# The second layer's convolution: five products over 113 rows become four over 128

## The reference

```
xz = jnp.einsum('bhwc,ec->bhwe', xp, in_proj_w)          # 48 -> 2 x 96
x_in, x_gate = jnp.split(xz, 2, axis=-1)
xc = conv_general_dilated(x_in, conv2d_w, (1, 1), 'SAME', feature_group_count=96)   # 3 x 3
x_act = jax.nn.silu(xc).reshape(B, H * W, 96)
ym = _mamba(x_act, ...)
ym = ym.reshape(B, H, W, 96) * jax.nn.silu(x_gate)
out = jnp.einsum('bhwd,cd->bhwc', ym, out_proj_w)

# in _mamba, after products that make u, z, dt, B and C:
da = jnp.exp(dt_t[..., None] * A)
h = da * h + (dt_t * x_t)[..., None] * B_t[:, None, :]
y = jnp.einsum('bdn,bn->bd', h, C_t)                     # then (y + xm * Dp) * silu(z), out_w
```

## Time and profile before

| | |
|---|---|
| median of 3 runs | 1626.08 us (1622.43 to 1626.56) |
| profiled execution | 1625.65 us |
| its span in the profile | 1623.8 us |
| TensorE (PE) busy | 1286.5 us, 79% |
| VectorE (DVE) busy | 1271.7 us, 78% |
| ScalarE (ACT) busy | 1154.7 us, 71% |
| GpSimd (POOL) busy | 898.3 us, 55% |
| pair products, `m_qf` L1499 | 192 instructions, 124.4 us busy, 799 ns each |
| scans, `m_h` L1729 | 384 instructions, 463.8 us busy, 53.4 us idle before them |

### The profile page before, as it was taken

How to read it: one execution, slowest core, us unless ns; L and a number is a source line. 1 busy time by engine, 2 the same in 40 slices (tenths; PEclk the granted TensorE clock), 3 DMA queues, 4 the chain that set the end, 5 groups by cost and what they waited for, 6 DMA issues and landing times. The chain is left out here.

```text
span 1623.8 us, 14529 instructions
## 1 busy us (share of the span) xinstructions
PE 1286.5 (79%) x3822; PEld 436.9 (27%) x3822; DVE 1271.7 (78%) x1274; ACT 1154.7 (71%) x1691; POOL 898.3 (55%) x451
## 2 busy tenths in 40 slices
PE   4999757585763577768789988998989889776995
PEld 2444201010110355532122222222222222111663
DVE  1665659999996477730999999999999999894775
ACT  2677358687773477748898898889898988641564
POOL 2400037969788333313987787888787888750000
PEclk8999955555555799978788889888897898555998
DMA  5344480200101233225877787777787877634572
GB/s 153 106 137 124 109 183 0 84 20 1 52 1 63 68 97 98 83 56 149 193 180 171 183 190 175 175 174 182 167 183 181 187 172 162 132 71 105 130 175 67
DMA packets 136429, 200.54 MB, mean 123 GB/s; under 512 B 26739, under 2 KB 68770, under 8 KB 135564
## 3 DMA queue, kind: packets, MB, share of 16 engines
q1 hardware_dynamic: 133740, 196.15, 49.5%
q10 hardware_dynamic: 2160, 2.61, 0.6%
q0 software_dynamic: 448, 0.85, 0.2%
HBM read 145.93 MB, written 53.63 MB: 123 GB/s over the span
## 5 line engine op out<-in xcount | busy, mean ns | idle before, releaser
L1375 POOL TENSOR_TENSOR m_ub<-m_dlb,m_bt 128x1536 f32<-128x1536 f32 x128 | 440.2, 3441 | 144.1 <-DVE m_h L1729 136.8
L1729 DVE TENSOR_TENSOR_SCAN m_h<-m_qa,m_state,m_ub 128x512 f32<-128x512 f32 x384 | 463.8, 1262 | 53.4 <-POOL m_ub L1375 51.9
L1691 ACT ACTIVATE m_qa<-m_dlb,k_a 128x512 f32<-128x512 f32 x384 | 254.8, 684 | 107.9 <-DVE m_h L1729 102.0
L1097 POOL TENSOR_TENSOR b_u<-b_dl,b_z 128x1024 f32<-128x1024 f32 x48 | 125.2, 2608 | 212.0 <-DVE b_dl L1014 211.4
L1740 DVE TENSOR_TENSOR m_g<-m_h,m_qc 128x1536 f32<-128x1536 f32 x128 | 221.7, 1732 | 14.3 <-issue 7.7
L1558 PE MATMUL m_qc<-m_bcr,k_selc 32*128 32x512 f32 x256 | 167.5, 738 | 81.8 <-DVE m_g L1740 81.6
L1575 PE MATMUL m_qy<-m_g,k_seld 128*32 128x512 f32 x768 | 169.5, 743 | 0.0
L944 PE MATMUL b_qb<-b_bc,k_pack_sel 96*128 96x512 bf16 x96 | 81.6, 850 | 73.6 <-DVE b_u L1020 71.0
L1499 PE MATMUL m_qf<-m_cva,k_conv 113*96 113x504 f32 (+1 forms) x192 | 124.4, 799 | 5.0 <-PEq L1131 5.0
L1558 PEld LDWEIGHTS m_qc<-m_bcr,k_selc 32*128 32x128 f32 x256 | 42.9, 209 | 205.7 <-issue 188.7
L983 ACT ACTIVATE b_qa<-b_dl,b_a 128x1024 f32<-128x1024 f32 x48 | 53.7, 1118 | 62.2 <-DVE b_dl L1014 62.2
(11 more groups left out here) (181 smaller groups left out, 2478.9 us busy)
## 6 DMA issues: line engine op xcount, KB each, us to landing
m_dlb<-scratch_dldu SPq DMA_DIRECT2D x128, 384.0 KB, 9.6
m_bt<-scratch_brow SPq DMA_DIRECT2D x128, 256.0 KB, 5.8
scratch_dldu<-m_dldu SPq DMA_DIRECT2D x32, 384.0 KB, 5.0
scratch_z<-a_z SPq DMA_DIRECT2D x24, 256.0 KB, 6.0
b_z<-scratch_z SPq DMA_DIRECT2D x3, 2048.0 KB, 11.4
scratch_y<-b_yrow SPq DMA_DIRECT2D x12, 512.0 KB, 2.6
c_y<-scratch_y SPq DMA_DIRECT2D x16, 384.0 KB, 3.4
scratch_gate<-m_gt SPq DMA_DIRECT2D x32, 192.0 KB, 4.8
```

The costliest lines, as they stand in the source:

```text
L1097: nc.gpsimd.tensor_tensor(by_column(u[s][:], col), by_column(dl[s][:], col), seen(z[j % 2][:], col, piece), ALU.mult).then_inc(u_ready, 1)
L1375: nc.gpsimd.tensor_tensor(ub[k % 3][:], dlb[u % 2][:, J:2 * J, :], bcast(bt[u % 2][:, n, :], J), ALU.mult).then_inc(ub_ready, 1)
L1691: nc.scalar.activation(q_a[:, j, :], dlb[u % 2][:, j, :], ACT.Exp, scale=G["a1"][:, j, n:n + 1]).then_inc(da, 1)
L1729: nc.vector.tensor_tensor_scan(h[k % 3][:, j, :], q_a[:, j, :], ub[k % 3][:, j, :], state[:, k % NS, j:j + 1], ALU.mult, ALU.add).then_inc ...
```

## The change

The tiles of a unit are filled differently, so that four products are left. `cva` now holds 48 channels of the middle row (partitions 0 to 47), 48 of the upper row (48 to 95) and the first 32 of the lower row (96 to 127). The three pair products contract over all 128 partitions. The last 16 channels of the lower row stand in `cvb` three times, in partitions 64 to 111, once for each shift by a column, and one low product over these 48 partitions serves the three taps. There is no left product, and the gate product reads partitions 0 to 47. Six transfers a unit take the place of four, and the waits on their semaphores count 96 for 64.

The weights follow: `conv1` has 128 partitions, `low1` lies in 64 to 111, `left1` is gone. Their inputs are eight more loads in ScalarE's list (`in1`, `dw1`, `in_low`). GpSimd makes a mask (`groups`, four memsets), TensorE three more small products (`ps_groups`), and VectorE makes `conv1` in `dve_make` and no longer in `dve_conv`.

The diff, cut to its core:

```diff
@@ Weights.__init__
+        self.in1, self.dw1 = m.sb("in1", [P, DI]), m.sb("dw1", [DI, 3, DI])
+        self.in_low, self.groups = m.sb("in_low", [64 + C, DI]), m.sb("groups", [DI, 3, 64 + C])
-        self.loads += [(G["gate64"][64:64 + C, :], D["pack_c"])]
+        self.loads += [(G["gate"][:], D["pack_c"])]
+        cin, cdw = (place("pack_cin", n) for n in ("c1_in", "c1_dw"))
+        for at, rows, of in ((0, C, 0), (C, C, 0), (2 * C, 32, 0)):
+            self.loads += [(self.in1[at:at + rows, :], D["pack_cin"][of:of + rows, cin])]
+        for at, of in ((0, 64), (C, 0)):
+            self.loads += [(self.dw1[at:at + C].rearrange("c k d -> c (k d)"), D["pack_cin"][of:of + C, cdw])]
+        for k in range(3):
+            self.loads += [(self.in_low[64 + LOW * k:64 + LOW * k + LOW, :], D["pack_cin"][32:C, cin])]
@@ pool_shape
+        nc.gpsimd.memset(self.groups[:], 0.0).then_inc(self.grouped, 1)
+        pool.wait_ge(self.grouped, 1)
+        for k in range(3):
+            nc.gpsimd.memset(self.groups[:, k, 64 + LOW * k:64 + LOW * k + LOW], 1.0).then_inc(self.grouped, 1)
@@ pe_bias
-            self.nc.tensor.matmul(self.ps_low[0:CIN, k, 0:DI], self.ones[:, 0:CIN], self.diag[:, k, :], start=True,
+            self.nc.tensor.matmul(self.ps_low[:, k, 0:DI], self.ones[:], self.diag[:, k, :], start=True,
+        pe.wait_ge(self.grouped, 4)
+        for k in range(3):
+            last = self.nc.tensor.matmul(self.ps_groups, self.groups[:, k, :], self.diag[:, k, :], start=(k == 0), stop=(k == 2))
@@ dve_conv, dve_make
-        for i in range(2):
-            self.nc.vector.tensor_tensor(self.G[f"conv{i}"][:], bcast(self.in_w[i][:], 3), self.dw[i][:],
+        self.nc.vector.tensor_tensor(self.G["conv0"][:], bcast(self.in_w[0][:], 3), self.dw[0][:],
-        for rows, k in ((slice(0, 64), 1), (slice(64, CIN), 2)):
-            nc.vector.tensor_tensor(G["low1"][rows], self.in_w[1][rows], self.ps_low[rows, k, 0:DI], ALU.mult).then_inc(made, 1)
-        nc.vector.tensor_tensor(G["left1"][:], self.in_w[1][0:C + 1], self.ps_low[0:C + 1, 0, 0:DI], ALU.mult).then_inc(made, 1)
+        nc.vector.tensor_tensor(G["conv1"][0:DI], bcast(self.in1[0:DI], 3), self.dw1[:], ALU.mult).then_inc(made, 1)
+        nc.vector.tensor_tensor(G["conv1"][DI:P], bcast(self.in1[DI:P], 3), self.ps_low[DI:P, :, 0:DI], ALU.mult).then_inc(made, 1)
+        nc.vector.tensor_tensor(G["low1"][64:64 + C], self.in_low[64:64 + C], self.ps_groups[64:64 + C], ALU.mult).then_inc(made, 1)
@@ load_cv_unit
-    eng.dma_start(cva[0:C + 1, :], xpad[b, :, row:row + ROWS + 2, :].rearrange("c r w -> c (r w)")).then_inc(loaded, 16)
...
+    for at, last, down in ((0, C, 1), (C, C, 0), (2 * C, 32, 2)):
+        eng.dma_start(cva[at:at + last, :], rows(0, last, down).rearrange("c r w -> c (r w)")).then_inc(loaded, 16)
+    for tap in range(3):
+        o, i = COLUMNS[tap]
+        at = 64 + LOW * tap
+        eng.dma_start(cvb[at:at + LOW, :].rearrange("c (r w) -> c r w", w=W)[:, :, o],
+                      rows(32, C, 2)[:, :, i]).then_inc(loaded, 16)
@@ mid1_phase, TensorE
-                src = cva[r][0:CIN, 0:CH].rearrange("c (r w) -> c r w", w=W)
+                src = cva[r][:].rearrange("c (r w) -> c r w", w=W)
-                nc.tensor.matmul(q_f[:], G["low1"][:], cvb[r][0:CIN, :], start=False, stop=False)
-                o, i = COLUMNS[0]
-                nc.tensor.matmul(out[:, :, o], G["left1"][:], src[0:C + 1, :, i], start=False, stop=True).then_inc(conv_mm, 1)
+                nc.tensor.matmul(q_f[:], G["low1"][64:64 + C, :], cvb[r][64:64 + C, :], start=False, stop=True).then_inc(conv_mm, 1)
-                nc.tensor.matmul(q_g[0:DI, :], G["gate64"][64:64 + C, :], cva[v % 2][64:64 + C, 0:CH], start=True,
+                nc.tensor.matmul(q_g[0:DI, :], G["gate"][:], cva[v % 2][0:C, :], start=True,
```

More of the change, by code:

```diff
@@ L51 @@
 LEAD = 4
+LOW = C - 32
 def done(i):
@@ L112, with __init__ @@
 class Weights:
-    def __init__(self, nc, m, D, G, ps, ps_dt, ps_low):
-        self.nc, self.D, self.G, self.ps_dt, self.ps_low = nc, D, G, ps_dt, ps_low
+    def __init__(self, nc, m, D, G, ps, ps_dt, ps_low, ps_groups):
+        self.nc, self.D, self.G, self.ps_dt, self.ps_low, self.ps_groups = nc, D, G, ps_dt, ps_low, ps_groups
         self.raw = m.sb("raw", [P, sum(width(columns) for _, columns in PACKS["pack_raw"][2])])
@@ L249, in pe_bias @@
         for k in range(3):
-            self.nc.tensor.matmul(self.ps_low[0:CIN, k, 0:DI], self.ones[:, 0:CIN], self.diag[:, k, :], start=True,
+            self.nc.tensor.matmul(self.ps_low[:, k, 0:DI], self.ones[:], self.diag[:, k, :], start=True,
                                   stop=True).then_inc(self.bias_mm, 1)
+        pe.wait_ge(self.grouped, 4)
+        for k in range(3):
+            last = self.nc.tensor.matmul(self.ps_groups, self.groups[:, k, :], self.diag[:, k, :], start=(k == 0), stop=(k == 2))
+        last.then_inc(self.bias_mm, 1)
     def dve_conv(self, dve):
         dve.wait_ge(self.early_loaded, 16 * len(self.early))
-        for i in range(2):
-            self.nc.vector.tensor_tensor(self.G[f"conv{i}"][:], bcast(self.in_w[i][:], 3), self.dw[i][:],
-                                         ALU.mult).then_inc(self.conv_made, 1)
+        self.nc.vector.tensor_tensor(self.G["conv0"][:], bcast(self.in_w[0][:], 3), self.dw[0][:],
+                                     ALU.mult).then_inc(self.conv_made, 1)
     def dve_make(self, dve):
@@ L586, in front0_phase @@
                     [bank(2, r) for r in range(2)])
-        weights = Weights(nc, m, D, G, qn[0][:, 0, 0:1], qn[0][0:DI, 0, P:P + DI], qn[0][:, 1:4, :])
+        weights = Weights(nc, m, D, G, qn[0][:, 0, 0:1], qn[0][0:DI, 0, P:P + DI], qn[0][:, 1:4, :],
+                          qn[0][0:64 + C, 0, 16:16 + DI])
         nst = 16 * (J + 2)
@@ L695, in convolve @@
                     pe.wait_ge(ready, SLOTS)
-                    pe.wait_ge(weights.conv_made, 2)
+                    pe.wait_ge(weights.conv_made, 1)
                 if b == 0:
@@ L1119, in load_cv_unit, with rows @@
     row = i * ROWS
-    eng.dma_start(cva[0:C + 1, :], xpad[b, :, row:row + ROWS + 2, :].rearrange("c r w -> c (r w)")).then_inc(loaded, 16)
-    eng.dma_start(cva[64:64 + C + 1, 0:CH],
-                  xpad[b, :, row + 1:row + 1 + ROWS, :].rearrange("c r w -> c (r w)")).then_inc(loaded, 16)
-    eng.dma_start(cvb[0:C + 1, :],
-                  xpad[b, :, row + 2:row + 2 + ROWS, :].rearrange("c r w -> c (r w)")).then_inc(loaded, 16)
-    eng.dma_start(cvb[64:64 + C + 1, :].rearrange("c (r w) -> c r w", w=W)[:, :, 0:W - 1],
-                  xpad[b, :, row + 2:row + 2 + ROWS, 1:W]).then_inc(loaded, 16)
+    def rows(first, last, down):
+        return xpad[b, first:last, row + down:row + down + ROWS, :]
+    for at, last, down in ((0, C, 1), (C, C, 0), (2 * C, 32, 2)):
[5 more added lines that the diff above has]
+                      rows(32, C, 2)[:, :, i]).then_inc(loaded, 16)
 def back0_phase(nc, D, G, sems, past):
@@ L1488, in conv_pairs @@
                 if v < 2:
-                    pe.wait_ge(cv_first[v], 64)
+                    pe.wait_ge(cv_first[v], 96)
                 else:
-                    pe.wait_ge(cv_loaded[r], 64 * (v // 2))
+                    pe.wait_ge(cv_loaded[r], 96 * (v // 2))
                 if v >= 1:
@@ L1504, in conv_low @@
                 r = v % 2
-                out = q_f[:].rearrange("d (r w) -> d r w", w=W)
-                src = cvb[r][:].rearrange("c (r w) -> c r w", w=W)
-                nc.tensor.matmul(q_f[:], G["low1"][:], cvb[r][0:CIN, :], start=False, stop=False)
-                o, i = COLUMNS[0]
-                nc.tensor.matmul(out[:, :, o], G["left1"][:], src[0:C + 1, :, i], start=False, stop=True).then_inc(conv_mm, 1)
+                nc.tensor.matmul(q_f[:], G["low1"][64:64 + C, :], cvb[r][64:64 + C, :], start=False, stop=True).then_inc(conv_mm, 1)
             def gate_of(v):
@@ L1904, in views @@
     return found
-KEPT = [("conv0", [CIN, 3, DI], F32), ("conv1", [CIN, 3, DI], F32),
-        ("low1", [CIN, DI], F32), ("left1", [C + 1, DI], F32), ("wdt", [DI + 1, P], F32), ("gate64", [64 + C, DI], F32), ("dmat", [DI, DI], F32),
+KEPT = [("conv0", [CIN, 3, DI], F32), ("conv1", [P, 3, DI], F32),
+        ("low1", [64 + C, DI], F32), ("wdt", [DI + 1, P], F32), ("gate", [C, DI], F32), ("dmat", [DI, DI], F32),
         ("seld", [P, 32], F32), ("selc", [P, NS, 32], F32), ("minus1", [P, 1], F32),
@@ L1941, in build @@
             if phase is back0_phase:
-                G["cva"] = [ahead.enter_context(nc.sbuf_tensor(f"m_cva{r}", [P, (ROWS + 2) * W], F32)) for r in range(2)]
+                G["cva"] = [ahead.enter_context(nc.sbuf_tensor(f"m_cva{r}", [P, CH], F32)) for r in range(2)]
                 G["cvb"] = [ahead.enter_context(nc.sbuf_tensor(f"m_cvb{r}", [P, CH], F32)) for r in range(2)]
```

6 lines of the change are left out of this document (3 added, 3 removed).

## The result

The changed kernel takes 1660.6 us (median of 4 runs, 1659.17 to 1661.67), the kernel before 1625.8 us beside it: a ratio of 1.0218 with a 95% interval of 1.02 to 1.0235, so it is slower by about 35 us, as forecast (1658 us). The profiled execution's span is 1657.4 us, 33.6 us more than the 1623.8 us of before.

| | before | after | moved by |
|---|---|---|---|
| first layer's last stage begins (VectorE's first sum over rows) | 532.3 us | 532.0 us | -0.3 |
| from there to the second layer's first scan | 240.1 us | 237.4 us | -2.7 |
| from the first scan to the last `m_yo` | 709.4 us | 743.0 us | +33.6 |
| from there to the end | 142.1 us | 145.0 us | +2.9 |

A forecast was written before the change was run, and what follows sets the result against it. VectorE's scans were taken to set the pace in the second layer's scan stage. 1625.65 + 28.5 (clock) - 1.8 (startup) + 5.0 + 1.2 (first phase) = 1658.6, some 1658 us; range 1618 to 1680 us.

The forecast's parts named there:

- What bounds the kernel, and where the saved time goes: Second layer's scan stage: VectorE's scans set the pace; TensorE's saved 1.03 us per unit lengthens its wait, direct worth 0 us.
- The clock: Scan stage: the longer wait before C's broadcast makes TensorE's clock fall in nearly all 27 units, 1.5 us each: +28.5 us.
- Startup of the stage: Before the second layer's first scan: without left the first convolutions are ready sooner, -1.8 us (bounds 0 and -2.0).
- Weights and loads in the first phase: First phase: eight more ScalarE loads, +5.0 us, and making the weights, +1.2 us; together +6.2 us.
- Loads of a unit: Scan stage: SyncE issues two more transfers per unit, 0.66 us, covered by its own waiting: 0 us, at most 18.
- the clock doesn't mind: Rival, scan stage: clock falls stay as they are whatever the wait's length, 1630 us; chance 0.17.
- Early falls ended in time: Rival, scan stage: clock falls early, is back before the pair products, VectorE loses its 12.0 us of waits: 1618 us; chance 0.13.
- Low and gate do overlap: Counters a rival: in TensorE's step 1 low and gate run one behind the other, no clock term, 1632 us; chance 0.05.

The follow-up runs named there:

- without left: The kernel before the change with its left product left out, one tap of the convolution missing from the result: 1640.4 us, ratio 1.0088.
- filled over 48 rows: Changed kernel with its low product run four times at quarter weights, all over 48 rows: 1648.2 us; with the first three over 112 rows: 1628.6 us.
- the kernel with the wide product in step 3: Changed kernel with low run twice, once over 112 rows (1624.7 us), that wide one moved from step 1 to step 3, behind the pair products: 1645.0 us.
- products that compute nothing: Extra unread products in the last four turns, added to the changed kernel with one wide and one narrow low product: 1621.2 us; to the filled one: 1616.5 us.
- the loads alone: The kernel before with the change's eight weight loads added to ScalarE's list, into tiles that nothing reads: 1627.2 us (one run).
- the kernel with the six loads and one wide product: Changed kernel with low run twice at half weights, the first over 112 rows, 64 of them zeros: 1624.7 us, ratio 0.9994.

## Why the prediction was right, step by step

**What bounds the kernel, and where the saved time goes.** Right: the saved time went straight into a wait (1.64 to 2.67 us, and 0.80 to 1.83 us behind a slow unit), and nothing was gained for it in the steady state.

**The clock.** The term was +28.5 us and measured +34.3 us (46.3 for 12.0). Of its factors, the number was 27 units and is 22; the price was 1.5 us and is 2.1 us, because I counted one wait per unit, step 3's, and 16 units have two: the clock falls so early there that step 2's broadcast of C is late as well. The two errors partly cancel.

The step behind the number was only half right. It said that the length of the wait decides, and that this wait is 2.67 us in all units; it is 2.67 us behind undisturbed units, one in five, and 1.83 us behind the others. And the length is not all: without left the waits were those of before, and the falls came in 16 units for ten. So the work that goes counts by itself, and rows count in it (1648.2 us filled over 48 rows, 1628.6 us over 112). That the longer wait counts too is what the kernel with the wide product in step 3 suggests (14 units for ten at the same work); how the two share the 34 us stays open, since no kernel here had the long wait with the old work in every unit.

What grew can be counted, in the one profiled execution of each kernel: slow units in a row, which the prediction did not consider. In the kernel before TensorE waits only 0.80 us behind a slow unit, and none of the ten units behind a slow one is slow. Without left, at the same 0.80 us, 8 of 15 are; with the wide product in step 3, at 1.83 us, 3 of 14; in the changed kernel, which has less work and 1.83 us, 16 of 21.

Why it comes in units of 24.1 us one after the other can be read in the five units above. A slow unit ends late, and the next fall finds the next unit at nearly the same place: counted from `m_yo`, by the trace's record of the granted clock, the slow stretches of the first three begin after 2.7, 2.5 and 2.3 us, of the fourth after 9.0 us, where it is harmless, of the fifth after 4.7 us.

The rule of the Trainium skill that I had set against this ("TensorE: Matmul & The Clock Gate", section "HAM oscillation — how this bites in real kernels": the clock falls where TensorE idles long enough between bursts) would have given 1630 us. The trace disagrees once more: behind waits of 1.83 us and with TensorE busy for 22.3 of 24.1 us the clock falls in every one of these units. The advice on the same page of the Trainium skill, section "Why this matters for your kernels", is to keep TensorE busy without a break. The end of the stage agrees with it (0.53 to 0.86 by products that compute nothing).

**Startup of the stage.** -1.8 us forecast, -2.7 us measured, within the profiles' spread; the first activation of the convolution came 1.8 us earlier.

**Weights and loads in the first phase.** This is the term that failed: +6.2 us forecast, -1.0 us measured at the end of the phase (202.3 to 201.3 us), and +0.1 us for the loads alone. ScalarE's issuing grew by 2.4 us (12.21 for 9.78), not by 3 to 7: the issues cost 0.5 us each, not 0.63, and those of `xp` behind them got shorter; above all, a start that is 2 us late was made good within 5 us, since GpSimd was later still. I had followed the path to the first tap and taken its delay for the phase's, without asking what else would be moved by it. Over the profiles of this study the phase ends between 199.0 and 204.5 us, so a term of 1 us there can't be told from nothing.

**Loads of a unit.** Right: 0 us. SyncE's own waiting, 23.8 us before, is still 14.8 us in 24 waits, and the kernel with the six loads and one wide product is as fast as before.

**The rivals.** That the clock doesn't mind is refuted by 22 units. Early falls ended in time in none of the 24.1 us units: the pair products take 3.96 us in the one shown. The kernel before has one unit in which such a fall did end in time, and the prediction missed it, though it is the unit of the earlier trace rows: its u product is slow, and its pair products take 2.79 us.

```profile
1199.15 2.02 PE L1538 MATMUL m_qm<-m_xa,k_pack_d 96*96 96x512 f32 x2
```

So of the 17 units that have the 1.64 us wait, ten have an early fall behind it and nine lose time; the tenth slow unit is the first, where the scans start. Low and gate do overlap. That the sum came out within 3 us of the measurement is luck: the clock term was 6 us too small and the first phase's 7 us too large.

## What to carry to other kernels

Where an engine waits, a product that is saved on it is worth nothing, and on TensorE it may cost: look at what the granted clock does behind its waits before taking work away there. A slow clock is paid for at the step with the least room, so moving work from that step into the wait (one pair product: 34 us back, no instruction more) is worth trying before filler; but the same move in the kernel before put the longest wait in front of a worse place and cost 18 us. And a delay at the start of a phase is not a delay of its end: look for what else is pushed back with it.

## What the runs showed of the hardware

- Two kernels with the same columns in the same places and, in undisturbed units, the same waits of TensorE differ by 20 us (1648.2 and 1628.6 us) when three products of a unit have 112 rows for 48, 64 of them zeros.
- Filling TensorE doesn't only help: at 0.96 of the clock thirteen units ran without a wait, and after a fall the same kernel was bound by TensorE for a unit at 0.64 (27.31 us for 21.36).
- VectorE's two taps took 5.23 us beside GpSimd's work and 1.51 us without it. The Trainium skill ("SBUF — State Buffer", section "SBUF: two separate sides") says that an instruction of VectorE with two operands in SBUF and one of GpSimd that reads SBUF exclude each other; the rows agree with it, but no run here was made to test it.
